# Four edits to a fused attention and feed-forward kernel: a cast moved to ScalarE, a rescaled second layer norm, another order of the GELU steps, and a later first load

## The reference

```python
q, k, v = X @ Wq.T + bq, X @ Wk.T + bk, X @ Wv.T + bv
s = where(j > i, -inf, q @ k.T / 32)
x = layernorm(X + softmax(s, axis=-2) @ v)      # over the query axis
h = x
for blk in range(3):
    y = qlora(h, 2*blk)                          # 1024x1024, dequantized, + rank 32
    y = gelu(layernorm(y) * gamma + beta)
    h = qlora(y, 2*blk + 1) + h
out = layernorm(x + h)
```

## Time and profile before

| | us |
|---|---|
| median of the 2 runs (2693.62 to 2695.81) | 2694.72 |
| the profiled execution | 2688.71 |
| its span on core 7, the slowest | 2687.1 |
| spans of the 8 cores | 2670.6 to 2687.1 |
| TensorE busy in matmuls (6880) | 1688.3 (63%) |
| ScalarE busy (1517) | 1035.8 (39%) |
| VectorE busy (1001) | 1028.6 (38%) |
| GpSimd busy (112) | 131.4 (5%) |

### The profile page before, as it was taken

The page is one execution under the profiler, slowest core; times in us unless marked ns, Lnnn a source line. Parts: engine busy times, 40 slices in busy tenths (PEclk is TensorE's granted clock), DMA queues, the critical chain, the costliest instruction groups (busy, mean ns, idle before and its releaser), DMA issues.

```text
span 2687.1 us, 21892 instructions; the slowest of 8 cores (2670.6 to 2687.1 us)
## 1 busy us (share of the span) xinstructions
PE 1688.3 (63%) x6880; PEld 695.6 (26%) x6880; DVE 1028.6 (38%) x1001; ACT 1035.8 (39%) x1517; POOL 131.4 (5%) x112
## 2 busy tenths in 40 slices
PE   0999891296989201114677746876477775676863
PEld 0444340142434000001223212332133221232321
DVE  2113534400352644443425532444524526152452
ACT  0421204243020413223564446446454564546444
POOL 0000002400000421010000000000000000000000
PEclk9999896698999655556888858988788887688985
DMA  6210034501002076767110042010141000511001
GB/s 195 93 36 17 33 124 142 202 16 55 16 26 101 0 243 233 252 234 249 32 63 32 1 125 94 32 63 1 42 147 63 32 32 0 188 33 62 32 1 63
DMA packets 72542, 228.62 MB, mean 85 GB/s; under 512 B 6768, under 2 KB 7024, under 8 KB 66032
## 3 DMA queue, kind: packets, MB, share of 16 engines
q1 hardware_dynamic: 61680, 181.09, 20.8%
q0 software_dynamic: 10752, 46.14, 4.4%
HBM read 181.07 MB, written 46.14 MB: 85 GB/s over the span
## 4 chain that ended last, share of the span: by engine, by line
PE 46%; ACT 17%; DMA 11%; DVE 11%; issue 10%; PEld 2%; DVEq 1%; PEldq 1%; SPq 0%; ACTq 0%; POOL 0%; POOLq 0%
PE ps L857 21%; PE ps L298 8%; PE ps L420 5%; PE ps L361 4%; DMA weffs<-PL 4%; ACT PL L1033 2%; PEld ps L496 2%; PE ps L837 2%; PE ps L1085 2%; DVE PL L1023 2%; DMA PL<-xt 2%; DVE PL L627 2%; DVE PL L624 2%; PE ps L839 2%; ACT L1007 2%
## 5 line engine op out<-in xcount | busy, mean ns | idle before, releaser
L857 PE MATMUL ps<-PL 128*128 128x512 bf16 x3072 | 770.7, 409 | 166.5 <-ACT PL L1033 80.3
L857 PEld LDWEIGHTS ps<-PL 128*128 128x128 bf16 x3072 | 317.0, 104 | 598.5 <-issue 292.5
L298 PE MATMUL ps<-PL 128*128 128x512 bf16 x1024 | 229.1, 387 | 171.4 <-DVE PL L214 64.0
L725 PE MATMUL ps<-PL 32*128 32x512 bf16 x48 | 28.2, 587 | 297.9 <-DVEq L748 200.6
L1001 DVE TENSOR_TENSOR e2s<-e2s,m2s 128x512 f32<-128x512 f32 x32 | 22.1, 691 | 472.9 <-ACT e2s L993 472.9
L880 ACT ACTIVATE PL<-ps,fb 128x512 bf16<-128x512 f32 x192 | 132.0, 687 | 163.1 <-PE ps L839 162.9
L298 PEld LDWEIGHTS ps<-PL 128*128 128x128 bf16 x1024 | 101.4, 100 | 298.5 <-issue 183.2
L1085 PE MATMUL ps<-eye,PL 128*128 128x128 f32 x256 | 86.9, 435 | 143.7 <-ACT PL L1099 78.7
L893 DVE SCALAR_TENSOR_TENSOR PL<-ps,fb,PL 128x512 f32<-128x512 f32 x192 | 143.8, 749 | 46.9 <-PE ps L857 46.5
L496 PE MATMUL ps<-PL 128*128 128x512 bf16 x640 | 143.0, 388 | 20.2 <-ACTq L173 20.2
L837 PE MATMUL ps<-PL,ones_b 128*128 128x512 bf16 x192 | 76.0, 396 | 117.5 <-ACT sqd L883 117.5
(11 more groups left out here) (80 smaller groups left out, 1725.1 us busy)
## 6 DMA issues: line engine op xcount, KB each, us to landing
PL<-weffs SPq DMA_DIRECT2D x24, 2048.0 KB, 9.4
PL<-xt SPq DMA_DIRECT2D x32, 1024.0 KB, 6.0
PL<-qw_t SPq DMA_DIRECT2D x48, 512.0 KB, 5.0
PL<-sc_t SPq DMA_DIRECT2D x48, 512.0 KB, 6.5
x1s<-PL POOLq DMA_DIRECT2D x16, 1024.0 KB, 10.6
PL<-x1s SPq DMA_DIRECT2D x64, 256.0 KB, 8.6
out<-PL POOLq DMA_DIRECT2D x32, 512.0 KB, 3.5
weffs<-PL POOLq DMA_DIRECT2D x48, 256.0 KB, 6.3
```

The costliest lines, as they stand in the source:

```text
L298: last = e.matmul(ps[bank][:], bfv(area + c * 512, 1024)[:, s * 128:(s + 1) * 128], xtbf[:, c * 2048 + tc * 512:c * 2048 + (tc + 1) * 512] ...
L857: last = e.matmul(ps[bank][:], bfv(WSL[sl], 8192)[:, c * 1024 + s * 128:c * 1024 + (s + 1) * 128], src_mv[:, c * 512:(c + 1) * 512], start ...
```

## The change

Four things are different.

1. The cast of sequence 1's xt moves from VectorE to ScalarE, and in ScalarE's queue it now stands ahead of the squares of sequence 0's first norm. SP's loads follow ScalarE's counter.
2. `ln2_apply` leaves the mean out: it multiplies the tile by 1/std and, in a second instruction of 512 columns, mean by 1/std (into e2s). `trans_store` transposes 9 instead of 8 pieces for each 128 tokens; the first is a piece of that product, of which ScalarE copies one column with factor -1 into m2s, and the eight copies become adds of that column.
3. `apply_gelu` of tile 0 is emitted after `ln_fin2` of tile 1 and no longer ahead of it, in all 12 blocks.
4. Load and cast of the first group's tile 0 are emitted after the dequantization.

```diff
+                @blk.sync
+                def _(e):
+                    wt(e, "pe", p2e)
+                    for c in range(EC):
+                        if c >= 2:
+                            wt(e, "se", pf_base + c - 1)
+                        inc(e.dma_start(out=pf_st[c % 2],
+                                        in_=xt[seq + 1, c * 128:(c + 1) * 128, :]),
+                            "lx%d" % (c % 2), 16)
+                @blk.scalar
+                def _(e):
+                    wt(e, "pe", p2e)
+                    for c in range(EC):
+                        wt(e, "lx%d" % (c % 2), pfl[c % 2] + 16 * (c // 2 + 1))
+                        inc(e.activation(bfv(O_XTBF + c * 1024, 2048),
+                                         pf_st[c % 2], AF.Copy), "se")
...
-            if seq + 1 < NSEQ:
-                pf_base = cnt["ve"]
...
-                @blk.vector
-                def _(e):
-                    wt(e, "pe", p2e)
-                    for c in range(EC):
-                        wt(e, "lx%d" % (c % 2), pfl[c % 2] + 16 * (c // 2 + 1))
-                        inc(e.tensor_copy(bfv(O_XTBF + c * 1024, 2048),
-                                          pf_st[c % 2]), "ve")
...
-                inc(e.tensor_sub(x3, h3, bc512(muB, i * 512)), "ve")
-                chain(e, "ve")
-                inc(e.tensor_mul(x3, x3, bc512(rsB, i * 512)), "ve")
+                inc(e.tensor_mul(x3, h3, bc512(rsB, i * 512)), "ve")
+                inc(e.tensor_mul(e2s[:, i * 512:(i + 1) * 512],
+                                 muB[:, i * 512:(i + 1) * 512],
+                                 rsB[:, i * 512:(i + 1) * 512]), "ve")
...
-                    for c in range(EC):
+                    for c in range(EC + 1):
...
-                        inc(e.copy(fv(36864 + tsl * 1024 + c * 128, 128),
-                                   ps[4 + n % 2][:, 0:128]), "se")
+                        if c == 0:
+                            inc(e.activation(m2s[:, i * 512:i * 512 + 1],
+                                             ps[4 + n % 2][:, 0:1],
+                                             AF.Copy, scale=-1.0), "se")
+                            chain(e, "se")
+                        else:
+                            inc(e.add(fv(36864 + tsl * 1024 + (c - 1) * 128, 128),
+                                      ps[4 + n % 2][:, 0:128],
+                                      m2s[:, i * 512:i * 512 + 1]), "se")
...
                     y_mms(t, w1, wl[w1], cm[t], "y1", fbcols[w1])
-                    if t != ts[0]:
-                        gel[ts[0]] = apply_gelu(ts[0], blki, fin[ts[0]])
                     fin[t] = ln_fin2(t)
                 for t in ts:
-                    if t not in gel:
-                        gel[t] = apply_gelu(t, blki, fin[t])
+                    gel[t] = apply_gelu(t, blki, fin[t])
...
-        xm0 = x1_load(0, (("ve", attn_end["ve"]),))
-        cm0 = cast_in(0, IBASE[0], xm0)
-
         scope("dequant")
```

More of the change, by code:

```diff
@@ L519, in build_program @@
             barrier()
+            if seq + 1 < NSEQ:
+                pf_base = cnt["se"]
+                pfl = [cnt["lx0"], cnt["lx1"]]
+                pf_st = [fv(O_VV, 2048), fv(O_VV + 2048, 2048)]
+                p2e = p2_pe[EC - 1]
+                @blk.sync
[14 more added lines that the diff above has]
+                                         pf_st[c % 2], AF.Copy), "se")
+                assert cnt["se"] == pf_base + EC
+                sqm["xpf"] = ("se", pf_base + EC)
             sqb = [O_SQ0, O_SQ1]
@@ L1110, in _ @@
                         in_=fv(36864 + tsl * 1024, 1024)), "sp", 16)
-            tr_idx["n"] += 32
+            tr_idx["n"] += 36
             inst_free_pe[i] = cnt["pe"]
@@ L1115, in build_program, with emit_group @@
         fbcols = [fb[:, w * 8:(w + 1) * 8] for w in range(6)]
-        def emit_group(gname, ts, ex_x1=None, ex_cast=None, hook=None,
-                       pre=None):
+        def emit_group(gname, ts, ex_x1=None, ex_cast=None, hook=None):
             nonlocal_osb = None
             scope(gname)
-            xm = dict((t, m[0]) for t, m in (pre or {}).items())
+            xm = {}
             wl = {}
-            cm = dict((t, m[1]) for t, m in (pre or {}).items())
+            cm = {}
             for j in (0, 1):
@@ L1126, in emit_group @@
                     hook(j)
-            if ts[0] not in xm:
-                xm[ts[0]] = x1_load(ts[0], (ex_x1 or {}).get(ts[0], ()))
+            xm[ts[0]] = x1_load(ts[0], (ex_x1 or {}).get(ts[0], ()))
             wl[0] = w_load(0)
@@ L1131, in emit_group @@
             for t in ts[1:]:
-                if t not in xm:
-                    xm[t] = x1_load(t, (ex_x1 or {}).get(t, ()))
+                xm[t] = x1_load(t, (ex_x1 or {}).get(t, ()))
             for t in ts:
-                if t not in cm:
-                    cm[t] = cast_in(t, IBASE[t % 2], xm[t],
-                                    extra=(ex_cast or {}).get(t, ()))
+                cm[t] = cast_in(t, IBASE[t % 2], xm[t],
+                                extra=(ex_cast or {}).get(t, ()))
             for blki in range(3):
@@ L1185, in build_program @@
         ygrp["guard"][5] = ("ve", dq_end["ve"])
-        ex0 = {1: (("se", dq_end["se"]), ("ve", dq_end["ve"]),
+        ex0 = {0: (("ve", attn_end["ve"]),),
+               1: (("se", dq_end["se"]), ("ve", dq_end["ve"]),
                    ("gq0", dq_end["gq0"]), ("gq1", dq_end["gq1"]),
```

33 lines of the change are left out of this document (11 added, 22 removed).

## The result

The changed kernel is slower: the ratio of its time to that of the kernel before is 1.0254, 95% interval [1.0229, 1.0279], on a median before of 2693.5 us. That is +68 us, about 2762. The profiled execution took 2757.66 us (span 2756.0 on core 0), the one of before 2688.71, +69.

The account below looks back on a forecast made before the run. TensorE held the chain for just under half of the span, stopping twice per block in y2. Terms 86 + 12.4 + 16 - 15 = +99 gave 2788 on 2688.7, or 2794 on the median; forecast 2791 us, range 2768 to 2823.

Parts of the forecast that it names:

- Edit 3, +86: Groups' blocks: y2 loses 32 matmuls done ahead and starts 0.2 later; 7.2 us per block, 12 blocks, +86 us.
- Two passes of VectorE stand between L1009 and the GELU's table load: Each block, before y2: tile 0's passes follow tile 1's ln_fin2 and take 9.2 us.
- The lower bound of 63: Groups' blocks: one slow start fewer in y2 takes off 1.9 us, leaving 5.3 per block, 63 us.
- Edit 1, +12.4: First norm: casts and squares on ScalarE run in a row, barrier at 453.2 against 440.8, +12.4 us.
- Edit 2, +16: Second norm at each group's end: earlier start, but 36 pieces and dearer adds; +3.9 us a group, four groups, +16.
- Edit 4, -15: Dequantization: entry saves 22 us at the third chunk, first weights at the end give back 7; net -15 us.
- A: Rival, blocks: y2 goes at VectorE's pace, so the late GELU order costs only 2 us; total 2704, chance 0.10.
- B: Rival, second norm: ScalarE's one-column copy and add need different function tables, 82 us more; total 2873, chance 0.02.
- D: Rival, dequantization: stores hold up the first chunks anyway, so moving the first load costs +7; total 2813, chance 0.07.
- C: Rival, second norm: long own-counter wait in each piece, costing its upper end of 48 us; total 2823, chance 0.07.

Follow-up runs that it names:

- e5_wait: Against the kernel before: tile 0's GELU steps behind tile 1's ln_fin2, plus a wait of tile 0's VectorE passes for tile 1's L1009; ratio 1.0324, +87 us.
- edit 2 alone: Against the kernel before: only the mean left out of ln2_apply, with 36 transposes and adds a tile; ratio 1.0066, +18 us.

## Why the prediction was right in direction and wrong in size

- **Edit 3, +86: wrong, 46 to 53.** The step that failed is "Two passes of VectorE stand between L1009 and the GELU's table load". That is true of tile 1's passes, from which I took the 9.55 us; tile 0's do not wait for L1009 of tile 1. They wait for tile 0's own `fin`, long given, and stand in VectorE's queue behind tile 1's L1001 alone, so they start 2.0 us before L1009 and not behind its end. Behind L1009 they do cost 87. By blocks it is 4.1 us and not 7.2. The form of the forecast was right: TensorE's last run starts near the time at which it started before, and what is lost is the 32 matmuls that were done ahead.
- **The lower bound of 63** failed with it. It did not vary the place of the passes, and the 1.9 us that it takes off for one slow start fewer should not come off at all: before, the first of the two slow starts lies ahead of a stop that another engine ends, and the last run starts slowly in both kernels. Leaving it out of the sum was right, as the 7.2 us per block of e5_wait show.
- **Edit 1, +12.4: right**, +12.7 at its barrier, 16 in the time.
- **Edit 2, +16: right**, 18 measured. Tile 0's first piece is copied out 10.5 us after L1009 instead of 14.4, 3.9 earlier (forecast 3.7), and the pair of adds takes 1.05 us (forecast 1.04). The forecast had put the difference of one add, 0.10, on a pair of two without giving a reason; it held because 0.08 of the 0.20 comes out of waits (10.4 us over 128 pairs). The 14.4 are 1571.84 less the start of L1009 in ScalarE's timeline of the kernel before:

```profile
1557.45 0.63 ACT L1009 ACTIVATE rsB<-m2s 128x512 f32<-128x512 f32 x1
```

- **Edit 4, -15: right**, -14.5. The third L739 is 19.8 us earlier (forecast 22), and the end gives 12.8 - 3.8 = 9.0 back in the mean over cores (forecast 7). The forecast weighed the rule of the Trainium skill, DMA: Bandwidth & Descriptors, section Queues, rings and completion order, that each DMA engine serves its queue rows in turn: with it 983, without it some 5 us sooner. Measured against the end of VectorE's last pass these are 23 and 18, and the row has 25.0. The trace agrees with the rule: SP's load L693, issued at 972.10, landed after 12.7 us, while the last store to x1s, issued before it at 971.10 in the other queue, took 21.9 us (13.86 before). That store landed 24.0 us after the last pass, against 975.84 - 959.83 = 16.0 before, so the drain was stretched by 8 us where the forecast had 5.8.
- **Rivals.** A (edit 3 costs nothing) fell: L893 waits 2.02 us for TensorE behind the passes, so TensorE sets the pace. (The 38 us from which A was to decide should be 54 - 13.4 = 41.) B fell by the single table load of a tile, D by the third L739. C (edit 2 at 48) fell by edit 2 alone, which costs 18.

## What to carry to other kernels

When an instruction is moved in a queue, write down what it waits for itself, apart from what stands ahead of it: a step whose inputs are ready starts with its turn, often ahead of the neighbour that the old trace shows before it. Ask of each half of a moved step on its own: the VectorE half of this one belonged early and the ScalarE half late, which together gave a gain where moving both gave a loss. And judge a stop that another engine ends by when TensorE starts its last run and by how much work is left then, and not by TensorE's waits or busy time alone: matmuls that run slowly ahead of such a stop only shorten it.
